# Another order of the operations inside the step of an adaptive-layernorm cross-attention kernel, on ScalarE, VectorE, GpSimd and the DMA queue

## The reference

```python
xq  = _ada_ln(x_q,  t_vec, Wss_q,  bss_q)       # layernorm, times (1+scale), plus shift
xkv = _ada_ln(x_kv, t_vec, Wss_kv, bss_kv)
q = (xq @ Wq + bq).reshape(B, Lq, nh, dh)
kv = (xkv @ Wkv + bkv).reshape(B, Lkv, 2, nh, dh)
scores = einsum("bqhd,bkhd->bhqk", q, k) / sqrt(dh)
attn = softmax(scores, axis=-1)
out = einsum("bhqk,bkhd->bqhd", attn, v).reshape(B, Lq, H)
return x_q + (out @ Wp + bp)
```

## Time and profile before

| what | value |
|---|---|
| median of 3 runs | 1081.02 us (1079.53 to 1083.94) |
| the profiled execution | 1089.12 us, its span 1087.3 us |
| PE busy | 1030.4 us (95%) |
| DVE busy | 986.7 us (91%) |
| ACT busy | 822.0 us (76%) |
| POOL busy | 830.3 us (76%) |

### The profile page before, as it was taken

How to read it: one execution, slowest core, us unless ns; L and a number is a source line. 1 busy time by engine, 2 the same in 40 slices (tenths; PEclk the granted TensorE clock), 3 DMA queues, 4 the chain that set the end, 5 groups by cost and what they waited for, 6 DMA issues and landing times.

```text
span 1087.3 us, 29139 instructions
## 1 busy us (share of the span) xinstructions
PE 1030.4 (95%) x10091; PEld 588.4 (54%) x10091; DVE 986.7 (91%) x1288; ACT 822.0 (76%) x1458; POOL 830.3 (76%) x933
## 2 busy tenths in 40 slices
PE   7989999999999999999999999999999999999975
PEld 4866555555555555555555555555555555555532
DVE  5665799999999999999999999999999999999984
ACT  3466588878788888878787888888787878887642
POOL 2253496978888797978788887979788888979554
PEclk8789999999999999999999999999999999999998
DMA  9321567767776676776766767767677676776665
GB/s 324 113 77 40 146 156 183 168 172 174 171 177 172 175 186 160 184 166 178 180 168 177 173 172 178 173 172 174 175 173 174 176 180 168 180 172 151 149 153 126
DMA packets 336402, 181.26 MB, mean 167 GB/s; under 512 B 277308, under 2 KB 283480, under 8 KB 336360
## 3 DMA queue, kind: packets, MB, share of 16 engines
q1 hardware_dynamic: 336336, 180.72, 66.3%
q10 hardware_dynamic: 24, 0.01, 0.0%
HBM read 77.90 MB, written 33.55 MB: 103 GB/s over the span
## 4 chain that ended last, share of the span: by engine, by line
PE 69%; ACT 9%; issue 7%; DVE 3%; POOL 1%; DMA 1%; SPq 1%; ACTq 0%; DVEq 0%; POOLq 0%
PE ps_q L1427 26%; PE ps_o L1484 23%; PE ps_s L1448 8%; PE ps_v L1468 8%; PE ps_v L1410 4%; ACT pr L711 2%; ACT kb L636 1%; ACT vb L658 1%; DVE oT_lo L1039 1%; ACT p L676 1%; ACT junk L702 1%; DVE p L1088 1%; DMA pt<-p 1%; ACT w_hi L719 1%; SPq L335 0%
## 5 line engine op out<-in xcount | busy, mean ns | idle before, releaser
L510 POOL TENSOR_TENSOR half_den<-pr 128x512 f32<-128x512 f32 x128 | 163.5, 1277 | 83.4 <-ACT pr L711 77.8
L503 POOL TENSOR_TENSOR xr<-y,xr 128x512 f32<-128x512 f32 x128 | 163.0, 1274 | 70.5 <-ACT y L646 68.7
L676 ACT CAST p<-ps_t 128x1024 f16<-128x1024 f32 x128 | 129.3, 1010 | 80.2 <-DVE ps_t L1064 78.3
L1072 DVE TENSOR_REDUCE mx<-ps_s 128x16 f32<-128x1024 f32 x128 | 156.7, 1224 | 26.2 <-PE ps_s L1448 23.8
L1088 DVE TENSOR_TENSOR p<-ps_t,p 128x1024 f16<-128x1024 f32 x128 | 156.4, 1222 | 12.7 <-ACT p L676 11.1
L479 POOL TENSOR_TENSOR xr<-xr,bp_row 128x512 f32<-128x512 f32 x128 | 163.2, 1275 | 0.0
L1064 DVE SCALAR_TENSOR_TENSOR ps_t<-pr,ps_v 128x1024 f32<-128x1024 f32 x128 | 155.5, 1215 | 0.3
L1080 DVE TENSOR_TENSOR pr<-ps_s,mx 128x1024 f32<-128x1024 f32 x128 | 155.3, 1214 | 0.0
L711 ACT ACTIVATE pr<-pr,exp_scale 128x1024 f32<-128x1024 f32 x128 | 146.2, 1142 | 10.6 <-DVE pr L1080 10.6
L687 ACT ACTIVATE q_hi<-ps_q,cur_bq 128x512 f16<-128x512 f32 x126 | 86.6, 688 | 87.8 <-PE ps_q L1427 87.2
L1484 PE MATMUL ps_o<-wp_hi,oT_hi 128*128 128x512 f16 x512 | 133.0, 383 | 14.5 <-DVE oT_lo L1039 14.5
(11 more groups left out here) (208 smaller groups left out, 1931.7 us busy)
## 6 DMA issues: line engine op xcount, KB each, us to landing
x_in<-in_x_dram SPq DMA_DIRECT2D x128, 256.0 KB, 3.1
xr<-in_x_dram SPq DMA_DIRECT2D x128, 256.0 KB, 3.0
out_dram<-xr SPq DMA_DIRECT2D x128, 256.0 KB, 2.9
pt<-p SPq DMA_TRANSPOSE x256, 3.2
raw<-in_L_xcond_Wss_kv_dram SPq DMA_DIRECT2D x4, 512.0 KB, 6.0
cx<-in_ctx_dram SPq DMA_DIRECT2D x4, 512.0 KB, 9.2
wss_q_raw<-in_L_xcond_Wss_q_dram SPq DMA_DIRECT2D x4, 512.0 KB, 11.0
raw<-in_L_xcond_Wkv_dram SPq DMA_DIRECT2D x2, 1024.0 KB, 11.2
```

The lines of the kernel that those rows point to most:

```text
L503: pool.tensor_tensor(xr[:, s, :], y[:, off % 2, :], xr[:, s, :], ALU.add).then_inc(y_ready, 1)
L510: pool.tensor_tensor(half_den[:, :, :], pr[:, off % 2, :, 0:LKV // 2], pr[:, off % 2, :, LKV // 2:LKV], ALU.add).then_inc(half_done, 1)
L1072: dve.tensor_reduce(mx[:, :], scores, AX_X, ALU.max).then_inc(mx_done, 1)
```

## The change

Every engine but TensorE gets another order inside its step. No instruction, size or wait condition of an operation changes. Some VectorE, ScalarE and GpSimd operations and the transfers change places:

```diff
@@ SP @@
             def step(b, i):
+                load_x(b, i + 12)
                 turn_p(b, i - 2, 0)
                 turn_p(b, i - 2, 1)
+                store(b, i - 4)
                 load_xr(b, i - 1)
-                store(b, i - 4)
-                load_x(b, i + 12)
@@ POOL @@
             def step(b, i):
-                residual(b, i - 4)
                 await_rows(b, i + 9)
                 half_sums(b, i - 1)
...
+                residual(b, i - 4)
+                normalise(b, i + 9)
                 add_rows(b, i - 4)
-                normalise(b, i + 9)
@@ ACT @@
             def step(b, i):
                 split_p(b, i - 2)
+                output(b, i - 4)
                 turned_o(b, i - 3)
-                output(b, i - 4)
+                sum_rows(b, i + 10)
                 if i == 4:
                     query_bias(b + 1)
-                sum_rows(b, i + 10)
+                sum_squares(b, i + 10)
                 query(b, i + 4)
-                turned_x(b, i + 8)
-                sum_squares(b, i + 10)
+                exponential(b, i)
+                if i == 7:
+                    key_blocks(b + 1)
                 if i == 2:
                     values(b)
-                exponential(b, i)
+                turned_x(b, i + 8)
                 if 2 <= i <= 5:
                     scaled_wq_hi(b + 1, i - 2)
-                if i == 7:
-                    key_blocks(b + 1)
@@ DVE @@
                 weight_sums(b, i - 1)
+                query(b, i + 4)
+                denominators(b, i - 1)
+                normalise_p(b, i - 1)
                 turned_x(b, i + 8)
-                denominators(b, i - 1)
-                query(b, i + 4)
-                normalise_p(b, i - 1)
```

## The result

The changed kernel takes 1094.42 us, the median of 4 runs (1090.24 to 1097.12); the kernel before, timed beside it, 1082.3 us. The ratio is 1.0109, 95% interval 1.0081 to 1.0137: slower by about 12 us, where +2.0 was forecast. The median lies 0.4 us above the forecast's range. The profiled execution took 1093.58 us, with a span of 1091.7.

The account below looks back on a forecast made before the run. TensorE was taken as the bound, VectorE with little room. Per batch, 1.85 us of stalls go and 1.99 return at weigh: 60.31 against 60.17, times 14 batches +2.0, so 1083.0 us; 8 in 10 range 1074 to 1094.

Parts of the forecast that it names:

- the stall behind step 2: TensorE's 0.58 us loss where vb ahead of the exponential makes turn_x wait for oT_lo; forecast to go.
- two heavy and three double steps: Batch's longest path: steps 2 and 7 at 7.88 us each, the other six as three pairs of 14.85; 60.31 us.
- X to W: From the start of xT_lo on VectorE to the weigh on TensorE that waits for it: forecast 0.83 us.
- M to X: VectorE, from the start of mx to the start of xT_lo, now last in the step: forecast 6.62 us, before 4.68.
- S to M: From the start of score on TensorE to the start of mx on VectorE: forecast 0.88 us.
- W to S: TensorE, from the start of weigh to the next score: forecast 6.52 us, unchanged.
- W to X: Steps 2 and 7, from weigh through q_hi, exponential, vb or kb, and xT_hi to xT_lo: forecast 7.05 us.
- Rival 1: VectorE's reciprocal result costs nothing extra in the loop, 0.16 us to ps_t: batch 59.89, time 1077 us; chance 0.12.
- Rival 2: weigh doesn't wait in ordinary steps, only steps 2 and 7 cost 0.59 each: batch 59.50, time 1072 us; chance 0.12.
- Rival 3: Transposes of p land late behind store, xr and x loads: 0.34 us per double step, +14 us, 1097; chance 0.19.
- the one given 0.12: Same mechanism as the forecast sum, with small delays at its eight hand-overs adding to over 5.4 us; chance 0.12.
- The likeliest case: The forecast sum as it stands, 1083.0 us, own range 1079 to 1088; chance 0.45.

Follow-up runs that it names:

- The runs with the wait on the matmul: Changed kernel with weigh's wait for xT_lo last (1081.83 us, ratio 1.0), or between its two waits for the transposed p (ratio 0.999).
- the run with both edits: Changed kernel with weigh's wait for xT_lo last and the reciprocal ahead of q_lo on VectorE: 1079.05 us, ratio 0.9966.

## Why the prediction was right or wrong

The bound and the mechanism were right. `kb` and the stall behind step 2 went; a wait of `weigh` for xT_lo came in their place, 65 times; the batch is two heavy and three double steps, and the difference of the batch times 14 gives the measured loss. What failed is the size of two terms in a sum whose parts nearly cancel (1.85 taken away, 1.99 put back, where 2.65 came back).

**X to W, "0.83 us behind the start of a VectorE operation of this size that it waits for"**, was the wrong term. It measured 0.93 in the double steps and 0.94 in the heavy ones. The row was of `turn_x` waiting for oT_lo, where one control instruction stands between the late wait and the matmul; in `weigh` there are two, and each costs 0.10. The runs with the wait on the matmul measured 0.74. The term occurs five times a batch: 3 x 0.10 + 2 x 0.11 = 0.52.

**M to X, 6.62**, measured 6.67, three times a batch: 0.15. Within it the reciprocal to `ps_t` was right (0.28, forecast 0.30), and q_lo to the reciprocal is 0.66, not the 0.60 borrowed from the row of xT_lo. Together 0.67, against the 0.66 that separate 60.31 from 60.97; S to M, W to S and the heavy steps' W to X are each within 0.01.

The heavy steps' W to X, 7.05, measured 7.04. The squares ahead of q_hi did cost nothing here, since q_hi still waits for TensorE (0.64 us at 524.07 in the changed kernel).

Rival 1 did not come: the dependent `ps_t` follows the reciprocal at 0.28, an independent operation at 0.16 to 0.17. The Trainium skill, "VectorE: DVE Perf Modes", "The DRAIN you can't avoid", reports from its own chain of copies that a semaphore costs nothing extra; the 0.12 between these two numbers doesn't agree with it, and the forecast was right to go by the row. Rival 2 did not come, as M to X is 0.3 over the limit. Rival 3's time was the nearest and its mechanism wrong: `pt` is waited for twice. The case that came is the one given 0.12, small delays at the hand-overs of the same mechanism, at the far end of it. The likeliest case's own range, 1079 to 1088, took in the reciprocal's bounds and put none on X to W, though that term comes five times a batch.

## What to carry to other kernels

Where two engines release each other in a ring, write the ring out step by step and multiply each term by how often it is crossed in the run: here 0.1 us counted 70 times. Take each hand-over from a row of the same receiving instruction, and count in the built program the control instructions from the one that carries the late wait to the engine's own instruction. The order of the waits in the code doesn't decide it: with the wait last in the code the matmul carried it in the loop, and an event semaphore did in the written-out steps. When an order is changed on several engines, time the parts alone: a part that looked harmful (xT_hi late) hid one that gained 1.5% with a small addition.

## What was not expected of the hardware

- TensorE starts 0.74 to 0.75 us behind the start of a 128x512 VectorE operation when its wait for it rides on the matmul, and 0.10 later for each control instruction from the one that carries the wait to the matmul: 0.83, 0.93, 1.03 for one, two, three.
- An operation that needs the result of the VectorE operation directly ahead of it starts 0.12 us later than one that doesn't: 0.28 against 0.16 behind the reciprocal, and 0.71 (the reciprocal) against mostly 0.59 (q_lo) behind den.
- q_lo lasts 0.74 to 0.75 us behind den, and the operation behind it follows at 0.66. Behind the reciprocal it mostly lasts 0.67 to 0.69, followed at 0.59 to 0.61, but in 11 of 94 steps of the run with both edits it lasts 0.75 there too. So the operation ahead of it isn't all that decides; why is open.
